# Bias rows fetched per tile and multiplied in four row tiles of TensorE, in an adaLN, scan and mixture-of-experts kernel

## The chip, the cores and the metric

The kernel runs on one core of one Trainium2 chip. The metric is the device time of one execution in microseconds. Five engines run their own instruction queues side by side: TensorE (PE, with its weight loads shown apart as PEld), VectorE (DVE), ScalarE (ACT), GpSimd (POOL), and SyncE (SP), which here only issues transfers. They are tied together by semaphores: an instruction that waits holds up everything behind it on its own queue.

## The reference

The input `x` is 16 batches of 512 tokens of 128 numbers. A first half normalises, modulates, runs a decaying scan and adds back; it takes the first 150 to 160 us of the kernel and is not touched by the change. The second half is a mixture of 8 experts with the best 2 per token:

```
h = jnp.einsum('td,edf->etf', xt, W1) + b1[:, None, :]
h = _layernorm(jax.nn.relu(h), g1, be1)
y = jnp.einsum('etf,efd->etd', h, W2) + b2[:, None, :]
y = _layernorm(jax.nn.relu(y), g2, be2)
gate = (jax.nn.one_hot(idx, E, dtype=x.dtype) * probs[..., None]).sum(axis=1)
out = jnp.einsum('te,etd->td', gate, y)
```

Here D = 128, F = 512, and `b1` is one row of 512 numbers per expert.

## The kernel before

Tokens are sorted by expert into rows in DRAM, and the second half runs over 135 expert tiles (`EXPERT_TILES`) of 128 rows, each of one expert. The code is a software pipeline written out by hand: `run_tiles` calls an `expert_step(s, n)` on each engine for s = 0, 1, 2, ..., and each engine does at step s a fixed list of jobs for tiles at different ages. The order of work on an engine is the order in which these lines are written. The jobs that matter here are these.

- **TensorE, step s.** `hidden(s)` makes h of tile s in a PSUM bank: a product of ones with `b1` (L1561), then three products of 512 columns (L1562 to L1564, high and low parts of activations and weights). Then it turns the rows of tile s+2 (L1553), makes y of tile s-4 in eight passes (L1672), and turns the activated h of tile s-2 in four (L1569).
- **ScalarE, step s.** It rounds tile s+1 (`h3hi`, L765), takes relu of h of tile s-1 (L769), relu of the normalised y of tile s-5 (`v`, L870), copies the turned h of tile s-3 (L773), and scales y of tile s-8 (`vs`, L878). In some steps it also works on finished batches (L845).
- **VectorE, step s.** It takes y of tile s-5 out of PSUM (`v0`, L1362), then does the normalisations, `h3lo`, statistics of h, and at the end the target rows of tile s (L1346).
- **GpSimd.** It adds the last shift to y of each tile (`add_shift`, L662, signals `y_ready`) and scatters the results by indirect transfers.
- **SyncE.** `load_next(i)` waits until tile i-8 has been turned and has its target rows, loads the rows of tile i (L504), and then calls `load_shifts(i - 6)`, which loads the three shift vectors of tile i-6, spread over all partitions (L515). Their buffers come round: up to tile 39 sixteen tiles later, from tile 40 on eight tiles later, and a load has to wait until GpSimd has used the buffer's last tile (the wait on `y_ready` in the lines below). Numbers of tiles and experts are loaded into registers four at a time.

```
def load_shifts(i):
    if i % AT_ONCE == 0:
        load_expert_numbers(i)
...
    if last_user(i) is not None:
        sp.wait_ge(y_ready, last_user(i) + 1)
    sp.dma_start(shift_rows[ring(i)], shifts_d[bass.ds(expert_of[i], 1), :].broadcast_to([P, 3 * D])).then_inc(shifts_loaded[shift_lane(i)], 16)
```

Before the change all of `b1` sits in SBUF (`b1_parts`, 128 partitions, high part in row 0, low part in row 1, the rest zeros written by eight ScalarE copies at the start, L747). PSUM holds h in banks 1 and 2, turned h in banks 3 and 0, y in banks 4 and 5, each pair used in turn, and turned rows in 6 and 7.

Of the kernel before, what the change touches and what calls it, by code (L numbers as in the profile page):

```python
# [6 lines left out]
def adaln_ssm_moe_kernel(nc, x_in, win_in, bin_in, bp_in, cp_in, dp_in, wout_in, bout_in, wr_in, br_in,  # L7
# [57 lines left out]
    gates_d = nc.dram_tensor("gate_b_rows", (1, B * D), F32, kind="Internal").ap()  # L65

    with ExitStack() as ctx:  # L67
# [3 lines left out]
        def sem(name):  # L71
            return ctx.enter_context(nc.semaphore(name))
# [46 lines left out]
        b1_parts = sb("b1_parts", [P, E, F], F32R)  # L119
# [160 lines left out]
        def last_user(i):  # L280

            return max((m for m in range(i) if ring(m) == ring(i)), default=None)

        early01 = [t[:].rearrange("p c l -> p (c l)").rearrange("p (j k) -> p j k", j=J) for t in xi]
# [28 lines left out]
        spare_stored = sem("spare_stored")  # L313
        pool_consts = sem("pool_consts")
        dve_setup, act_setup, pe_setup = sem("dve_setup"), sem("act_setup"), sem("pe_setup")
        gb_stored, gb_loaded, b1_stored = sem("gb_stored"), sem("gb_loaded"), sem("b1_stored")

# [18 lines left out]
        sums_done, sums_copied, sums_stored, sums_loaded, w2_ready = (  # L336
            sem("sums_done"), sem("sums_copied"), sem("sums_stored"), sem("sums_loaded"), sem("w2_ready"))
# [74 lines left out]
        def _(sp):  # L412
# [41 lines left out]
            sp.dma_start(sums_d, w2_sums).then_inc(sums_stored, 16)  # L454
            sp.dma_start(shifts_d[:, 0:D].rearrange("(o e) d -> o e d", o=1), w2_sums[0:1, :, :]).then_inc(shifts_stored, 16)
            sp.wait_ge(sums_stored, 16)
            sp.wait_ge(shifts_stored, 16)
# [3 lines left out]
            sp.wait_ge(act_setup, 3)  # L461
            sp.dma_start(b1_parts[0:1, :, :].bitcast(F32), b1hi.bitcast(F32)).then_inc(b1_stored, 16)
            sp.dma_start(b1_parts[1:2, :, :].bitcast(F32), b1lo[:].bitcast(F32)).then_inc(b1_stored, 16)

            sp.wait_ge(dve_setup, SETUP_PADDING)
            for n in range(NSPARE):
                sp.dma_start(rows_d[SPARE + n * P:SPARE + (n + 1) * P, :], padding[:]).then_inc(spare_stored, 16)
# [6 lines left out]
            sp.wait_ge(shifts_stored, 48)  # L474
# [3 lines left out]
            AT_ONCE = 4  # L478
            row_of, expert_of = {}, {}
# [95 lines left out]
            for i in range(ROUND1, EXPERT_TILES):  # L575
                if i == LAST_ROWS:
                    sp.wait_ge(spare_stored, 16 * NSPARE)
                    sp.wait_ge(padding_stored, 16 * E)
# [162 lines left out]
        def _(act):  # L741
# [3 lines left out]
            act.wait_ge(dve_setup, SETUP_PADDING)  # L745
            for e in range(E):
                ins = nc.scalar.activation(b1_parts[:, e, :], padding[:, TAGS:TAGS + 1].broadcast_to([P, F]), ACT.Copy)  # L747
            ins.then_inc(act_setup, 1)
# [18 lines left out]
            def hidden(i):  # L767
                act.wait_ge(h_done, i + 1)
                nc.scalar.activation(r[i % DEPTH], bank[1 + i % 2][:], ACT.Relu).then_inc(r_ready, 1)  # L769

            def hidden_turned(i):
                act.wait_ge(tr_done, i + 1)
                nc.scalar.activation(rT[i % DEPTH], bank[3 * (1 - i % 2)][:], ACT.Copy).then_inc(rT_ready, 1)  # L773
# [82 lines left out]
            def expert_step(s, n):  # L856
                q = n % 2
                if on(s + 1, EXPERT_TILES) and s + 1 >= EARLY_H:
                    high_part(s + 1, bank[7 - q][:, 0:P])
                if s == 1:  # L860
                    half_gates()
                if on(s - 1, EXPERT_TILES) and s - 1 >= EARLY_H:
# [24 lines left out]
                if s == EXPERT_TILES + 4:  # L887
                    late_y0g(EARLY, range(HALF, J))
# [27 lines left out]
        def _(dve):  # L916
# [52 lines left out]
            def gains_setup():  # L969
# [5 lines left out]
                dve.wait_ge(act_setup, 3)  # L975
# [381 lines left out]
            def values(s, q, p):  # L1357
# [4 lines left out]
                vec.scalar_tensor_tensor(wide(v0[p]), wide(bank[4 + p][:, 0:D]), rse[q][:, 0:1],  # L1362
# [135 lines left out]
        def _(pe):  # L1498
# [55 lines left out]

            def hidden(i):
                e, q = expert_of[i], i % 2
                h = bank[1 + q][:].rearrange("p (o f) -> p o f", o=1)
# [8 lines left out]
            def turn_hidden(i):  # L1566
                pe.wait_ge(r_ready, i + 1)
                for ch in range(CF):
                    ins = tr(bank[3 * (1 - i % 2)][:, ch * P:(ch + 1) * P], r[i % DEPTH][:, ch * P:(ch + 1) * P], ident[:])  # L1569
                ins.then_inc(tr_done, 1)  # L1570
# [83 lines left out]
            def expert_step(s, n):  # L1654
# [7 lines left out]
                if on(s - 4, EXPERT_TILES):  # L1662
                    e4 = expert_of[s - 4]
                    acc = bank[4 + q][:, 0:D].rearrange("p (o d) -> p o d", o=1)
# [70 lines left out]
```

## Time and profile before

| what | value |
|---|---|
| three timed runs | 515.19 to 515.96 us, median 515.49 us |
| profiled execution, first to last instruction (span) | 512.1 us |
| TensorE busy | 486.5 us, 95% of the span |
| VectorE busy | 440.3 us, 86% |
| ScalarE busy | 420.4 us, 82% |
| GpSimd busy | 364.3 us, 71% |
| mean granted TensorE clock | 0.985 of full speed |

The profile page gives no time for the profiled execution apart from its span; the 3.4 us between the span and the median of the timed runs lie outside the first and the last instruction. Busy shares are means over the whole kernel, so they are to be read by stage. Numbers of lines are those of the kernel before, except where rows of the change are shown.

### The profile page before, as it was taken

To read this page: it belongs to the slowest core of one execution; us is meant where nothing else is said; L and a number is where in the kernel's file an instruction comes from. 1 tells how busy PE (TensorE), PEld (TensorE's weight loads), DVE (VectorE), ACT (ScalarE), POOL (GpSimd) and SP (SyncE) were. 2 spreads that over 40 slices of the span, in tenths; PEclk is the share of its full clock that TensorE was granted. 3 is DMA by queue.
4 is the path that set the end of the run, shared out by engine and by line. 5 is a ranking of instruction groups with operands and counts; after the bars stand their busy time and mean duration, and the time that the engine had idled before them with its cause. 6 is when DMAs were issued, how large, how long until landed. Compare 5 with 4: busy or idle time off the path is not lost. (4 is left out here: it accounts for less than half of the span.)

```text
span 512.1 us, 14684 instructions
## 1 busy us (share of the span) xinstructions
PE 486.5 (95%) x3051; PEld 386.3 (75%) x3051; DVE 440.3 (86%) x2217; ACT 420.4 (82%) x1148; POOL 364.3 (71%) x483
## 2 busy tenths in 40 slices
PE   7989999999985899999999999999999999999994
PEld 6446656555544798998989799998999989999951
DVE  7779899998887698888888799988989999898894
ACT  6678887978764688888888798899989889999883
POOL 1004665666667778888888888888888888888871
PEclk9999999999997899999999999999999999999998
DMA  6980111145111789677515785677677677567555
GB/s 166 312 240 27 44 47 48 47 131 111 55 44 52 166 154 172 188 191 198 163 64 158 187 221 152 184 205 176 164 207 191 162 189 206 151 187 214 164 173 164
DMA packets 79786, 77.78 MB, mean 152 GB/s; under 512 B 11150, under 2 KB 72745, under 8 KB 79702
## 3 DMA queue, kind: packets, MB, share of 16 engines
q1 hardware_dynamic: 71286, 59.92, 47.2%
q0 software_dynamic: 8416, 16.93, 9.2%
q8 instruction: 29, 0.48, 0.3%
q14 instruction: 55, 0.45, 0.3%
HBM read 54.65 MB, written 22.59 MB: 151 GB/s over the span
## 5 line engine op out<-in xcount | busy, mean ns | idle before, releaser
L646 POOL DMA_INDIRECT expert_rows<-rows_ring,slot x128 | 123.3, 963 | 93.6 <-issue 76.3
L674 POOL DMA_INDIRECT expert_results<-y,target x119 | 123.0, 1034 | 30.7 <-issue 26.2
L1672 PE MATMUL bank<-W,h2T 128*128 x720 | 95.4, 275 | 0.8 <-ACT h2T L773 0.3
L1672 PEld LDWEIGHTS bank<-W,h2T 128*128 128x128 f32 x720 | 87.7, 192 | 9.1 <-issue 1.4
L870 ACT ACTIVATE v<-wmod 128x128 f32<-128x128 f32 x135 | 42.0, 311 | 39.1 <-DVE vg L1373 35.5
L1362 DVE SCALAR_TENSOR_TENSOR wmod<-bank,rse,shifts 128x128 f32<-128x128 f32 x119 | 41.6, 350 | 30.8 <-PE bank L1672 25.9
L1561 PE MATMUL bank<-b_parts,onesr 128*128 x135 | 64.9, 481 | 1.2 <-DVE h3lo L1140 1.2
L758 ACT ACTIVATE n<-X,nm,rs 128x128 f32<-128x128 f32 x128 | 54.1, 486 | 8.0 <-DVE nm L1307 8.0
L1145 DVE BATCH_NORM_STATS2 stf<-h1T 128x6 f32<-128x512 f32 x90 | 59.2, 658 | 0.0
L1569 PE MATMUL bank<-ident_wr,h1T 128*128 128x128 f32 x360 | 54.5, 274 | 0.0
L1562 PE MATMUL bank<-W1hi,h3hi 128*128 x135 | 53.8, 399 | 0.0
L1563 PE MATMUL bank<-W1lo,h3hi 128*128 x135 | 53.7, 398 | 0.0
L1564 PE MATMUL bank<-W1hi,h3lo 128*128 x135 | 53.6, 397 | 0.0
L769 ACT ACTIVATE h1T<-bank 128x512 f32<-128x512 f32 x90 | 53.0, 589 | 0.2 <-PE bank L1564 0.2
L773 ACT ACTIVATE h2T<-bank 128x512 f32<-128x512 f32 x90 | 52.3, 581 | 0.1
L1672 PE MATMUL bank<-W,third_rT 128*128 x360 | 47.6, 275 | 0.8 <-ACT third_rT L773 0.8
L1672 PEld LDWEIGHTS bank<-W,third_rT 128*128 128x128 f32 x360 | 43.7, 192 | 4.9 <-issue 1.0
L1569 PEld LDWEIGHTS bank<-ident_wr,h1T 128*128 128x128 f32 x360 | 42.9, 142 | 0.3 <-issue 0.2
L1373 DVE SCALAR_TENSOR_TENSOR vg<-v,mve,shifts 128x128 f32<-128x128 f32 x119 | 42.5, 357 | 0.0
L882 ACT ACTIVATE sde<-mve,eps 128x2 f32<-128x2 f32 (+1 forms) x138 | 40.6, 295 | 0.9 <-DVE mve L1386 0.7
L1140 DVE TENSOR_TENSOR h3lo<-bank,h3hi 128x128 fp32r<-128x128 f32 x135 | 37.9, 281 | 2.8 <-ACT h3hi L765 2.8
L1381 DVE BATCH_NORM_STATS2 sty<-v 128x6 f32<-128x128 f32 x135 | 38.0, 281 | 0.3 <-ACT v L870 0.2
(250 smaller groups left out, 1229.0 us busy)
## 6 DMA issues: line engine op xcount, KB each, us to landing
shifts<-expert_shifts SPq DMA_DIRECT2D x119, 192.0 KB
hrow<-expert_rows SPq DMA_DIRECT2D x135, 65.0 KB
xi<-expert_results SPq DMA_DIRECT2D x12, 512.0 KB, 5.3
out_x<-X SPq DMA_DIRECT2D x15, 256.0 KB
X<-in_L_attn_x SPq DMA_DIRECT2D x7, 512.0 KB, 7.4
W1lo<-in_L_ffn_W SPq DMA_DIRECT2D x4, 512.0 KB, 6.7
expert_rows<-rows_ring,slot POOLq DMA_INDIRECT x128
expert_results<-y,target POOLq DMA_INDIRECT x119
```

The source lines that it names most:

```text
L646: nc.gpsimd.indirect_dma_start(out=rows_d, out_offset=bass.IndirectOffsetOnAxis(ap=slot[q][:, n // TOPK, n % TOPK:n % TOPK + 1], axis=0), ...
L674: nc.gpsimd.indirect_dma_start(out=results_d, out_offset=bass.IndirectOffsetOnAxis(ap=target[i % TARGETS][:], axis=0), in_=y[k], in_offset ...
L758: ins = nc.scalar.activation(dst[:, j:j + 1, :], X[:, bass.ds(b * J + j, 1), :], ACT.Identity, bias=nm_[:, x_tiles + j:x_tiles + j + 1], s ...
L769: nc.scalar.activation(r[i % DEPTH], bank[1 + i % 2][:], ACT.Relu).then_inc(r_ready, 1)
L773: nc.scalar.activation(rT[i % DEPTH], bank[3 * (1 - i % 2)][:], ACT.Copy).then_inc(rT_ready, 1)
L1145: vec.bn_stats(stf[i % 2][:], r[i % DEPTH]).then_inc(stf_ready, 1)
L1561: mm(h, onesr[:], b1_parts[:, bass.ds(e, 1), :], start=True, stop=False)
L1562: mm(h, h3hi[i % DEPTH], W1hi[:, bass.ds(e, 1), :], start=False, stop=False)
L1563: mm(h, h3hi[i % DEPTH], W1lo[:, bass.ds(e, 1), :], start=False, stop=False)
L1564: mm(h, h3lo[i % DEPTH], W1hi[:, bass.ds(e, 1), :], start=False, stop=True).then_inc(h_done, 1)
L1569: ins = tr(bank[3 * (1 - i % 2)][:, ch * P:(ch + 1) * P], r[i % DEPTH][:, ch * P:(ch + 1) * P], ident[:])
L1672: ins = mm(acc, rT[(s - 4) % DEPTH][:, ch * P:(ch + 1) * P], W2[:, bass.ds(e4 * CF + ch, 1), :], start=(ch == 0), stop=(ch == CF - 1))
```

## The change

The two rows of `b1` of a tile (high and low part) no longer stay in SBUF. They are kept in a DRAM table `b1_d`, and each tile's two rows come by a transfer of its own into `b1_ring`, at partition 0, 32, 64 or 96 and one of two turns. The four bias products of four tiles (i to i+3, i a multiple of four) are issued one behind the other at the start of tile i, each with two rows only, in four row tiles of the array and into four h banks (1, 2, 3, 0). Turned h has one bank (4), y one bank (5). ScalarE takes relu ahead of the rounding copy in every fourth step. The zero copies at the start go, and a few semaphores are merged.

```diff
+        b1_ring = sb("b1_ring", [P, 2, F], F32R)
...
+        hidden_banks = [bank[n] for n in (1, 2, 3, 0)]
...
+        turned_bank, value_bank = bank[4], bank[5]
...
+            def load_b1(i):
+                if i == 0:
+                    sp.wait_ge(b1_stored, 32)
+                if i >= 2 * TOGETHER:
+                    sp.wait_ge(h_done, i - 2 * TOGETHER + 1)
+                for n in together(i):
+                    part, turn = b1_rows(n)
+                    sp.dma_start(b1_ring[part, turn, :].bitcast(F32), b1_d[bass.ds(expert_of[n], 1), :, :].rearrange("o k f -> (o k) f")
+                                 ).then_inc(b1_loaded[turn], 16)
+
             def load_shifts(i):
                 if i % AT_ONCE == 0:
                     load_expert_numbers(i)
-                if i == SLOTS:
-                    sp.wait_ge(b1_stored, 32)
+                if i % TOGETHER == 0:
+                    load_b1(i)
                 if last_user(i) is not None:
                     sp.wait_ge(y_ready, last_user(i) + 1)
...
-            for e in range(E):
-                ins = nc.scalar.activation(b1_parts[:, e, :], padding[:, TAGS:TAGS + 1].broadcast_to([P, F]), ACT.Copy)
...
+                last_of_group = s % TOGETHER == 0
+                if last_of_group and on(s - 1, EXPERT_TILES) and s - 1 >= EARLY_H:
+                    hidden(s - 1)
                 if on(s + 1, EXPERT_TILES) and s + 1 >= EARLY_H:
                     high_part(s + 1, bank[7 - q][:, 0:P])
...
+            def biases(i):
+                pe.wait_ge(b1_loaded[i // TOGETHER % 2], b1_count(i))
+                pe.wait_ge(r_ready, i)
+                for n in together(i):
+                    part, turn = b1_rows(n)
+                    mm(hidden_bank(n)[:], onesr[part, :], b1_ring[part, turn, :], start=True, stop=False)
...
-                if i >= 2:
-                    pe.wait_ge(r_ready, i - 1)
-                mm(h, onesr[:], b1_parts[:, bass.ds(e, 1), :], start=True, stop=False)
...
+                pe.wait_ge(rT_ready, i)
...
-                    if on(s - 6, EXPERT_TILES):
-                        pe.wait_ge(v0_ready, s - 5)
+                    if on(s - 5, EXPERT_TILES):
+                        pe.wait_ge(v0_ready, s - 4)
```

On SyncE the queue in the later tiles, where every fourth step loads four expert numbers (`experts`), reads like this before the change; `hrow` are a tile's rows, `shifts` its shift vectors.

```order
L515 DMA shifts<-expert_shifts 128x384
L504 ISA [waits target_ready,t3_done]
L504 DMA hrow<-expert_rows 128x130
L490 TENSOR_LOAD experts
L515 ISA [waits y_ready]
L515 DMA shifts<-expert_shifts 128x384
```

With the change four loads into `b1_ring` stand in the same place, behind the shift load of the tile before (with its wait on `y_ready`) and behind the row load of six tiles ahead.

```order
L549 ISA [waits y_ready]
L549 DMA shifts<-expert_shifts 128x384
L528 ISA [waits target_ready,t3_done]
L528 DMA hrow<-expert_rows 128x130
L514 TENSOR_LOAD experts
L539 ISA [waits h_done]
L539 DMA b_ring<-b_two_parts 2x512
L539 ISA
L539 DMA b_ring<-b_two_parts 2x512
L539 ISA
L539 DMA b_ring<-b_two_parts 2x512
```

The fourth such load and the tile's own shift load follow. So the loads for tiles i to i+3 are issued after the shift load of tile i-1.

On TensorE one tile begins like this before the change: the turns of the tile two steps back (L1569), the bias product, the products with `W1`.

```order
L1569 MATMUL bank<-ident_wr,h1T 128x128 [waits r_ready]
L1569 MATMUL bank<-ident_wr,h1T 128x128 x3
L1561 ISA [waits r_ready,h3lo_ready]
L1561 MATMUL bank<-b_parts,onesr 128x512
L1562 REGISTER_ALU
L1562 MATMUL bank<-W1hi,h3hi 128x512
```

With the change every fourth tile begins with four bias products that wait for the loads and for the relu of all tiles before, and the other three tiles begin with the products of `W1`.

```order
L1611 MATMUL bank<-ident_wr,h1T 128x128 [waits rT_ready,r_ready]
L1611 MATMUL bank<-ident_wr,h1T 128x128 x3
L1593 MATMUL bank<-b_ring,onesr 128x512 [waits r_ready,b1_loaded0]
L1593 MATMUL bank<-b_ring,onesr 128x512 x3
L1603 ISA [waits h3lo_ready]
L1603 MATMUL bank<-W1hi,h3hi 128x512
```

The first of the four carries the wait on `b1_loaded`, which counts all four loads of the group.

## Rows read from the trace of the kernel before

**Rows 1.** The page: span, and the busy time of the engines.

```profile
span 512.1 us, 14684 instructions
...
PE 486.5 (95%) x3051; PEld 386.3 (75%) x3051; DVE 440.3 (86%) x2217; ACT 420.4 (82%) x1148; POOL 364.3 (71%) x483
```

**Rows 2.** Waits of the engines, whole kernel: engine, line, releaser, us, times, longest.

```profile
DVE wmod L1362 <- PE bank L1672: 29.6, 72, 1.4
```

**Rows 3.** Timeline of TensorE, one step (tile 58) and the next bias: start, us, what.

```profile
302.69 0.47 PE L1561 MATMUL bank<-b_parts,onesr 128*128 x1
...
303.00 0.39 PE L1562 MATMUL bank<-W1hi,h3hi 128*128 x1
...
303.24 0.40 PE L1563 MATMUL bank<-W1lo,h3hi 128*128 x1
...
303.81 1.06 PE L1672 MATMUL bank<-W,h2T 128*128 x8
...
305.06 0.48 PE L1561 MATMUL bank<-b_parts,onesr 128*128 x1
```

**Rows 4.** Timeline of the other engines around the same step.

```profile
301.44 1.06 PE L1672 MATMUL bank<-W,third_rT 128*128 x8
...
302.54 0.35 DVE L1362 SCALAR_TENSOR_TENSOR wmod<-bank,rse,shifts 128x128 f32<-128x128 f32 x1
...
304.00 0.39 ACT L878 ACTIVATE wmod<-vg,rse 128x128 f32<-128x128 f32 x1
...
304.27 0.24 DVE L1346 TENSOR_SCALAR target<-hrow,tile_e 128x1 int32<-128x1 f32 x1
...
304.48 0.45 POOL L662 TENSOR_TENSOR y<-wmod,shifts 128x128 f32<-128x128 f32 x1 [0.40 <-ACT wmod L878]
...
305.04 0.59 ACT L769 ACTIVATE h1T<-bank 128x512 f32<-128x512 f32 x1
```

**Rows 5.** Waits of SyncE's queue, whole kernel: line, releaser, us, times, longest.

```profile
SPq L515 <- POOL y L662: 96.4, 85, 9.9
SPq L521 <- DVE target L1346: 74.8, 27, 47.1
```

**Rows 6.** Timeline of SyncE's transfers, in the later tiles.

```profile
305.08 0.33 SPq L515 DMA_DIRECT2D shifts<-expert_shifts  x1
305.65 0.33 SPq L504 DMA_DIRECT2D hrow<-expert_rows  x1
```

**Rows 7.** Timeline of SyncE's transfers, in the earlier tiles.

```profile
208.31 0.33 SPq L504 DMA_DIRECT2D hrow<-expert_rows  x1
209.15 0.33 SPq L515 DMA_DIRECT2D shifts<-expert_shifts  x1
210.65 0.33 SPq L504 DMA_DIRECT2D hrow<-expert_rows  x1
211.17 0.33 SPq L515 DMA_DIRECT2D shifts<-expert_shifts  x1
```

**Rows 8.** DMA issues: transfer, count, KB each, median us from issue to landing.

```profile
y<-in_L_c SPq DMA_DIRECT2D x1, 8.0 KB, 1.5
...
boutc<-in_L_attn_bout SPq DMA_DIRECT2D x1, 0.5 KB, 2.2
...
expert_rows<-padding SPq DMA_DIRECT2D x15, 65.0 KB, 3.0
```

**Rows 9.** Windows of TensorE: us, busy us (count), granted clock, DMA share, GB/s.

```profile
152.40:155.90 3.50, 0.93 (x11) 0.50 0.15 49
155.90:159.40 3.50, 3.50 (x12) 0.54 0.18 59
159.40:160.40 1.00, 0.76 (x5) 1.00 0.20 67
```

**Rows 10.** Timeline of TensorE at the end of the first half; in brackets the idle time before.

```profile
151.07 0.66 PE L1539 MATMUL bank<-ident_wr,mixT_both 128*128 128x128 f32 x4 [1.93 <-ACT mixT_both L820]
```

**Rows 11.** Waits of ScalarE in the first 30 us, from the timeline.

```profile
10.49 0.78 ACT L805 ACTIVATE h1T<-bank,mod 128x512 f32<-128x512 f32 x1 [1.27 <-DVE gb_raw L966]
```

More of the change, by code:

```diff
@@ L65, in adaln_ssm_moe_kernel @@
     gates_d = nc.dram_tensor("gate_b_rows", (1, B * D), F32, kind="Internal").ap()
+    b1_d = nc.dram_tensor("b1_two_parts", (E, 2, F), F32, kind="Internal").ap()
     with ExitStack() as ctx:
@@ L118, in adaln_ssm_moe_kernel @@
         b1hi = third_rT[0:E, :]
-        b1_parts = sb("b1_parts", [P, E, F], F32R)
+        TOGETHER = 4
+        QUARTER = P // TOGETHER
+        b1_ring = sb("b1_ring", [P, 2, F], F32R)
         onesr = sb("onesr", [P, P], F32R)
@@ L282, in last_user, with together, b1_rows, b1_count @@
             return max((m for m in range(i) if ring(m) == ring(i)), default=None)
+        def together(i):
+            return range(i, min(i + TOGETHER, EXPERT_TILES))
+        def b1_rows(i):
+            first = i % TOGETHER * QUARTER
+            return slice(first, first + 2), i // TOGETHER % 2
+        def b1_count(i):
+            return 16 * sum(len(together(n)) for n in range(i % (2 * TOGETHER), i + 1, 2 * TOGETHER))
+        hidden_banks = [bank[n] for n in (1, 2, 3, 0)]
+        def hidden_bank(i):
+            return hidden_banks[i % len(hidden_banks)]
+        turned_bank, value_bank = bank[4], bank[5]
         early01 = [t[:].rearrange("p c l -> p (c l)").rearrange("p (j k) -> p j k", j=J) for t in xi]
@@ L316, in adaln_ssm_moe_kernel @@
         gb_stored, gb_loaded, b1_stored = sem("gb_stored"), sem("gb_loaded"), sem("b1_stored")
+        b1_loaded = [sem(f"b1_loaded{n}") for n in range(2)]
         (n1_ready, t1_done, h1T_ready, xi0_done, xi1_done, xi0_ready, xi1_ready, z_done,
@@ L453, in _ @@
             sp.wait_ge(sums_copied, 2)
-            sp.dma_start(sums_d, w2_sums).then_inc(sums_stored, 16)
+            sp.dma_start(sums_d, w2_sums).then_inc(shifts_stored, 16)
             sp.dma_start(shifts_d[:, 0:D].rearrange("(o e) d -> o e d", o=1), w2_sums[0:1, :, :]).then_inc(shifts_stored, 16)
-            sp.wait_ge(sums_stored, 16)
-            sp.wait_ge(shifts_stored, 16)
+            sp.wait_ge(shifts_stored, 32)
             sp.dma_start(means[:, 0:E, :], sums_d[1:2].broadcast_to([P, E, D])).then_inc(sums_loaded, 16)
             sp.wait_ge(dve_setup, SETUP_END)
-            sp.wait_ge(act_setup, 3)
-            sp.dma_start(b1_parts[0:1, :, :].bitcast(F32), b1hi.bitcast(F32)).then_inc(b1_stored, 16)
-            sp.dma_start(b1_parts[1:2, :, :].bitcast(F32), b1lo[:].bitcast(F32)).then_inc(b1_stored, 16)
+            sp.wait_ge(act_setup, 2)
+            sp.dma_start(b1_d[:, 0, :], b1hi.bitcast(F32)).then_inc(b1_stored, 16)
+            sp.dma_start(b1_d[:, 1, :], b1lo[:].bitcast(F32)).then_inc(b1_stored, 16)
             sp.wait_ge(dve_setup, SETUP_PADDING)
             for n in range(NSPARE):
-                sp.dma_start(rows_d[SPARE + n * P:SPARE + (n + 1) * P, :], padding[:]).then_inc(spare_stored, 16)
+                sp.dma_start(rows_d[SPARE + n * P:SPARE + (n + 1) * P, :], padding[:]).then_inc(padding_stored, 16)
             for n, src in ((0, g2_in), (1, be2_in)):
@@ L473, in _ @@
                 sp.dma_start(shifts_d[:, (1 + n) * D:(2 + n) * D], second_gains[n]).then_inc(shifts_stored, 16)
-            sp.wait_ge(shifts_stored, 48)
+            sp.wait_ge(shifts_stored, 64)
             sp.wait_ge(w1lo_ready, E)
@@ L478, in _ @@
             AT_ONCE = 4
+            assert TOGETHER == AT_ONCE
             row_of, expert_of = {}, {}
@@ L576, in _ @@
                 if i == LAST_ROWS:
-                    sp.wait_ge(spare_stored, 16 * NSPARE)
-                    sp.wait_ge(padding_stored, 16 * E)
+                    sp.wait_ge(padding_stored, 16 * (NSPARE + E))
                     rows_of_batches(B)
@@ L861, in expert_step @@
                     half_gates()
-                if on(s - 1, EXPERT_TILES) and s - 1 >= EARLY_H:
+                if not last_of_group and on(s - 1, EXPERT_TILES) and s - 1 >= EARLY_H:
                     hidden(s - 1)
@@ L974, in gains_setup @@
                 assert done[0] == SETUP_SUMS
-                dve.wait_ge(act_setup, 3)
+                dve.wait_ge(act_setup, 2)
                 mark(vec.tensor_tensor(b1lo[:], b1f[:], b1hi, ALU.subtract))
@@ L1553, in turn_rows @@
                 tr(to, hrow[row_slot][:, H], ident[:]).then_inc(t3_done, 1)
-            def hidden(i):
-                e, q = expert_of[i], i % 2
-                h = bank[1 + q][:].rearrange("p (o f) -> p o f", o=1)
+            def biases(i):
[4 more added lines that the diff above has]
+                    mm(hidden_bank(n)[:], onesr[part, :], b1_ring[part, turn, :], start=True, stop=False)
+            def hidden(i):
+                e = expert_of[i]
+                h = hidden_bank(i)[:].rearrange("p (o f) -> p o f", o=1)
+                if i == 0:
+                    pe.wait_ge(h3lo_ready, EARLY_H)
+                if i % TOGETHER == 0:
+                    biases(i)
                 pe.wait_ge(h3lo_ready, i + 1)
-                if i >= 2:
-                    pe.wait_ge(r_ready, i - 1)
-                mm(h, onesr[:], b1_parts[:, bass.ds(e, 1), :], start=True, stop=False)
                 mm(h, h3hi[i % DEPTH], W1hi[:, bass.ds(e, 1), :], start=False, stop=False)
```

17 lines of the change are left out of this document (7 added, 10 removed).

## The prediction

> **What bounds the kernel now.** I read the page first: TensorE is busy 95% of the span, the others less [rows 1]. Then the waits: VectorE waits for TensorE's y in 72 tiles, 29.6 us in all [rows 2], so the tile phase runs at TensorE's pace and the other engines follow it. Then the timeline of one step: from one bias product to that of the next tile 302.69 to 305.06, 2.37 us [rows 3], and the 135 tiles keep that step almost throughout. A group of four tiles takes 9.48 us. What the change touches besides TensorE is SyncE's queue, so I read its waits too: it is not idle in the sense of being early. Its shift loads wait 85 times for GpSimd's add, 96.4 us in all, and its row loads 27 times for the target rows of VectorE [rows 5]. So whatever is put into this queue behind these waits is issued at their pace, not ahead of it. Until now that did no harm: shift vectors are used five steps later, rows six.
>
> **What it saves on TensorE.** The bias product costs 302.69 to 303.00, 0.31 us, of which 0.07 is the weight load that any first product after the turns pays (the next product follows after 0.24, 303.00 to 303.24) [rows 3]. So a step without it takes 2.37 - 0.24 = 2.13. Each group adds once a cost c for the four bias products. No row shows row tiles. From below c is one product, 0.24; from above it is four, one behind the other, 0.95, and twice the part of a product that goes on after the next has started (0.39 - 0.24 = 0.15, [rows 3]) if the array is emptied on both sides: 1.25. I take c = 0.45, one product and three more exposed weight loads of 0.07, nearer the lower end because the four have separate rows and banks. Then the group is 4 x 2.13 + 0.45 = 8.97 of TensorE, 0.5 less than now.
>
> The Trainium skill (TensorE: Matmul & The Clock Gate, Measured speedup vs the span model) has four row tiles of 32 rows and 512 columns at 3.07 times the speed of four in a row; c would be 0.95 / 3.07 = 0.31 by it and the sum 33 x 0.14 = 5 us less. Against the change speaks the Trainium skill (TensorEngine Tiling (Array Packing), Key Properties): changing the tiling mode drains TensorE. With both drains priced at 0.15 on top of 0.45 the sum would be 33 x 0.30 = 10 us more.
>
> **What it adds: the loads of b1 come late.** The four loads of group S (tiles S to S+3) stand behind the row load of tile S+6 and the shift load of tile S-1, and the first product of step S waits for all four. I follow the chain from the start of one group to that of the next.
>
> From tile 40 on the shift load of tile S-1 waits for the add of tile S-9, which ScalarE and GpSimd do late in their step S-1. In the rows: y of step 57 ends at 301.44 + 1.06 = 302.50, VectorE takes it at 302.54, ScalarE scales at 304.00, GpSimd adds at 304.48 [rows 4], and the shift load of tile 58 leaves at 305.08 [rows 6], when TensorE starts tile 59 (305.06, [rows 3]). Behind it: 0.57 to the row load (305.08 to 305.65, [rows 6]); 0.84 from there to the next transfer where expert numbers are read in between (208.31 to 209.15), and 0.52 from one issue to the next (210.65 to 211.17) for three more loads [rows 7]; and the landing of the last. Landing from issue: 1.5 us for 8 KB, 2.2 for 0.5 KB, 3.0 for 65 KB [rows 8]. These loads are 4 KB; I take 2.2 and keep 1.5 and 3.0 for the range. From the start of group S to the end of y in step S+2: c, two steps of 2.13, and 302.69 to 303.81 + 1.06 less 0.24, 1.94 [rows 3], together 6.20 + c = 6.65. Then 302.50 to 305.08, 2.58; then 0.57 + 0.84 + 3 x 0.52 = 2.97; then 2.2. The sum is 14.40 us from group to group, against 9.48 now. TensorE has 8.97 of work in it and stands for 5.4.
>
> Up to the group of tile 40 the shift buffers come round after sixteen tiles and their wait is over; what holds the queue is the row load of tile S+6, which waits for the target rows of tile S-2. That is one step earlier: 4.07 + c = 4.52 to the end of y in step S+1; 302.50 to the end of the target rows at 304.51 is 2.01 [rows 4], and 0.15 to the load (as from GpSimd's add, 304.93, to the shift load); then 0.84 + 1.56 and 2.2. Together 11.28, with 2.3 us of standing.
>
> **The clock.** After an idle stretch of 1.93 us [rows 10] the granted clock went to 0.50, 1.2 GHz, and stayed there for 3.5 us after TensorE was at work again, 155.9 to 159.4, before it was 1.00 [rows 9]. At half clock 3.5 us do the work of 1.75. A stand of 5.4 us is well beyond that; I charge 1.8 per group. For 2.3 us I charge half, 0.9, since one row of that size is no proof for all. Behind these rows stands the Trainium skill (TensorE: Matmul & The Clock Gate, HAM oscillation — how this bites in real kernels): a wait for a transfer in every tile makes every tile begin at the lower clock. Were that so for the early groups too, they would lose 1.8 each and the sum be 9 us more.
>
> **What costs nothing.** The relu wait: a group needs relu of tile S-1, which runs 305.04 to 305.63 beside a bias at 305.06 [rows 3, 4]; 0.5 us late if the loads were early, hidden wholly behind a stand of 2.3 or 5.4, and if the loads were in time it would be the next wait. The single banks for turned h and y wait for copies that end during the stand as well. The eight zero copies at the start sit before a wait of ScalarE for VectorE of 1.27 us [rows 11], so their going frees nothing. The wait on `h_done` in front of the loads is for a tile eight back, long done. The extra bytes, 4 KB per tile, are small beside 65 KB of rows and the shift vectors.
>
> **The sum.** Groups 4 to 40 are 10, groups 44 to 132 are 23; group 0 is loaded long before. Late groups: 14.40 + 1.8 - 9.48 = 6.72, times 23 is 154.6. Early groups: 11.28 + 0.9 - 9.48 = 2.70, times 10 is 27. Together 181.6 us on a span of 512.1, or on the median of 515.5 (3.4 us lie outside the span and stay): **697 us**.
>
> **The rivals.**
> - *The loads are late, but the clock holds.* For it: one row of a fall after a short stand is little, and 8.97 us of dense work stand between the stands. Without the clock the sum loses 23 x 1.8 + 10 x 0.9 = 50: 647 us.
> - *The clock stays down for whole groups.* Then 6.65 of the chain doubles in late groups (4.85 more each than charged), and in early groups TensorE's 8.97 doubles to 17.9 and sets the pace itself (5.7 more each): 112 + 57, 866 us. Against it: after 3.5 us of steady work the clock came back [rows 9].
> - *Dearer pieces.* Landing at 3.0 adds 33 x 0.8 = 26; c at 1.25 adds 33 x 0.8 = 26: 723 each, 749 both. Landing at 1.5 takes 23 off.
> - *The loads are in time.* Then it is not slower. That decides itself at one point: the last load must land before the first product of step S, some 5 us earlier than the chain gives, which needs the adds of GpSimd two steps earlier than in rows 4 and 6. Then the group is 8.97 and the relu wait of 0.45, 9.42 against 9.48: 33 x 0.06, 513.5 us, no change. The 85 waits of rows 5 speak against it.
>
> **Chances and range.** The forecast 0.55, clock holds 0.18, dearer pieces 0.16, clock down for good 0.08, in time 0.03. A difference under 0.2% can't be told from none here; faster gets 0.01, same 0.02, slower 0.97. The range takes the forecast, the clock that holds with short landings (down to 630) and the dear pieces together (up to 755), and leaves out the last two.
>
> **What would show it.** TensorE waits before the first bias product of nearly every group, some 2 us in early groups and 5 in late ones, released by the `b1_ring` loads; steps are about 2.1 within a group; SyncE's shift loads still wait for GpSimd; the granted clock falls after the stands; the bias group itself is short, about 0.45. The forecast is wrong if the loads land before the group, if their landing is far from 2.2 us, or if the clock does not fall.

## The result and the profile after

The changed kernel takes 700.21 us (median of four runs, 696.45 to 703.36), the kernel before 515.34 us beside it on the same chip (four runs, 514.96 to 515.96). The ratio is 1.358, with a 95% interval of 1.354 to 1.362. The profiled execution has a span of 698.7 us, 186.6 more than before, and a mean granted TensorE clock of 0.867 against 0.985.

The page of the changed kernel answers to [rows 1] and says at once that no engine got more work. TensorE and VectorE are busy for 63 and 1 us more, in a span that is 187 us longer:

```profile
span 698.7 us, 14981 instructions
PE 549.2 (79%) x3051; PEld 424.2 (61%) x3051; DVE 441.2 (63%) x2217; ACT 419.0 (60%) x1140; POOL 360.3 (52%) x483
```

The waits of the changed kernel (engine, line, releaser, total us, times, longest) answer to [rows 2] and [rows 5]. First TensorE, then VectorE, then SyncE's queue:

```profile
PE bank L1593 <- DMA b_ring<-b_two_parts: 126.5, 33, 6.7
DVE wmod L1395 <- PE bank L1714: 214.6, 86, 9.4
SPq L549 <- POOL y L695: 208.5, 68, 8.7
```

TensorE waits 33 times, once for every group but the first, for the new loads. 126.5 us of these waits and 63 us more of busy time make up the 187 us to within 3 us. The count of instructions is that of before, so the 63 us are the same work done slower. SyncE still waits for GpSimd's add, 208.5 us instead of 96.4, and VectorE for TensorE: everything stands in one ring.

The timeline of TensorE over one late group, from the bias products of tile 92 to those of tile 96 (start, us, engine, line, operation; in brackets the idle time before and its releaser):

```profile
499.74 0.80 PE L1593 MATMUL bank<-b_ring,onesr 2*128 2x512 f32 x4 [4.35 <-DMA b_ring<-b_two_parts]
500.47 0.80 PE L1603 MATMUL bank<-W1hi,h3hi 128*128 x1
...
504.55 0.78 PE L1603 MATMUL bank<-W1hi,h3hi 128*128 x1
...
507.59 0.48 PE L1603 MATMUL bank<-W1hi,h3hi 128*128 x1
...
508.48 1.06 PE L1714 MATMUL bank<-W,h2T 128*128 x8
...
509.73 0.47 PE L1603 MATMUL bank<-W1hi,h3hi 128*128 x1
...
516.77 0.80 PE L1593 MATMUL bank<-b_ring,onesr 2*128 2x512 f32 x4 [4.65 <-DMA b_ring<-b_two_parts]
```

and SyncE's transfers in the same stretch, which answer to [rows 6]:

```profile
512.25 0.33 SPq L549 DMA_DIRECT2D shifts<-expert_shifts  x1
512.82 0.33 SPq L528 DMA_DIRECT2D hrow<-expert_rows  x1
513.66 1.57 SPq L539 DMA_DIRECT2D b_ring<-b_two_parts  x4
...
515.00 0.24 SPq L539 DMA_DIRECT2D b_ring<-b_two_parts  x1
```

The last row, from a narrower window, is the fourth of the b1 loads by itself. The order is the one foretold: y of step S+2 (508.48 + 1.06 = 509.54), the add, the shift load at 512.25, the row load, the four b1 loads, and 1.77 us after the last of them was issued TensorE's next group. The windows of TensorE in this group (us, busy us and count, granted clock, DMA share, GB/s) answer to [rows 9]:

```profile
499.70:503.60 3.90, 3.86 (x15) 0.50 0.30 66
503.60:507.20 3.60, 3.60 (x19) 0.60 0.00 0
507.20:512.10 4.90, 4.90 (x38) 1.00 0.56 145
512.10:516.77 4.67, 0.02 (x2) 1.00 0.80 258
```

The first two steps, 4.08 and 3.04 us (500.47, 504.55, 507.59), run wholly or for the greater part at half clock; the third is 2.14.

An early group begins otherwise. The timeline of TensorE, tiles 20 and 24:

```profile
227.35 0.51 PE L1593 MATMUL bank<-b_ring,onesr 2*128 2x512 f32 x4 [1.53 <-DMA b_ring<-b_two_parts]
227.79 0.50 PE L1603 MATMUL bank<-W1hi,h3hi 128*128 x1
...
230.85 1.05 PE L1714 MATMUL bank<-W,third_rT 128*128 x8
...
238.05 0.51 PE L1593 MATMUL bank<-b_ring,onesr 2*128 2x512 f32 x4 [1.42 <-DMA b_ring<-b_two_parts]
```

and SyncE's in front of the second of them:

```profile
234.12 0.33 SPq L528 DMA_DIRECT2D hrow<-expert_rows  x1
234.96 1.75 SPq L539 DMA_DIRECT2D b_ring<-b_two_parts  x4
...
236.30 0.41 SPq L539 DMA_DIRECT2D b_ring<-b_two_parts  x1
```

All ten early groups (tiles 4 to 40) start their bias products at full clock (0.50 or 0.51 us for the four) after stands of 1.3 to 2.5 us; of the 23 late ones (tiles 44 to 132), after stands of 4.0 to 6.7 us, 20 take 0.80, the duration at half clock, and three 0.64 to 0.66.

### The profile page after: what moved, and what is told of

Its sections match the earlier page's. It is cut to its first block and busy times, and to the rows that moved or that the text cites. A ratio compares the mean times of both kernels' runs of the same rounds, so it can differ in the third digit from the quotient of the medians.

```text
span 698.7 us, 14981 instructions
## 1 busy us (share of the span) xinstructions
PE 549.2 (79%) x3051; PEld 424.2 (61%) x3051; DVE 441.2 (63%) x2217; ACT 419.0 (60%) x1140; POOL 360.3 (52%) x483
## 5 line engine op out<-in xcount | busy, mean ns | idle before, releaser
L1593 PE MATMUL bank<-b_ring,onesr 2*128 2x512 f32 x135 | 23.8, 689 | 126.5 <-DMA b_ring<-b_two_parts 126.5
L795 ACT ACTIVATE h3hi<-bank 128x128 fp32r<-128x128 f32 x135 | 35.9, 267 | 135.8 <-PE bank L1586 135.6
L1714 PE MATMUL bank<-W,h2T 128*128 x720 | 110.5, 304 | 0.5 <-DVE wmod L1395 0.4
L1714 PEld LDWEIGHTS bank<-W,h2T 128*128 128x128 f32 x720 | 103.0, 220 | 11.7 <-issue 6.0
L1593 PEld LDWEIGHTS bank<-b_ring,onesr 2*128 2x128 f32 x135 | 8.6, 244 | 134.7 <-DMA b_ring<-b_two_parts 132.7
L1603 PE MATMUL bank<-W1hi,h3hi 128*128 x135 | 79.5, 589 | 0.6 <-DVE h3lo L1173 0.6
L695 POOL TENSOR_TENSOR y<-wmod,shifts 128x128 f32<-128x128 f32 x58 | 28.5, 493 | 88.0 <-ACT wmod L911 87.7
L1604 PE MATMUL bank<-W1lo,h3hi 128*128 x135 | 63.2, 468 | 0.0
L1605 PE MATMUL bank<-W1hi,h3lo 128*128 x135 | 62.3, 461 | 0.0
L695 POOL TENSOR_TENSOR y<-win,shifts 128x128 f32<-128x128 f32 x28 | 13.9, 496 | 84.6 <-ACT win L911 84.5
```

The lines of the kernel that those rows point to most:

```text
L695: nc.gpsimd.tensor_tensor(wide(y[k]), wide(vs[i % VS]), wide(shift_rows[k][:, 2 * D:3 * D]), ALU.add).then_inc(y_ready, 1)
L1603: mm(h, h3hi[i % DEPTH], W1hi[:, bass.ds(e, 1), :], start=False, stop=False)
L1604: mm(h, h3hi[i % DEPTH], W1lo[:, bass.ds(e, 1), :], start=False, stop=False)
L1605: mm(h, h3lo[i % DEPTH], W1hi[:, bass.ds(e, 1), :], start=False, stop=True).then_inc(h_done, 1)
L1714: ins = mm(acc, rT[(s - 4) % DEPTH][:, ch * P:(ch + 1) * P], W2[:, bass.ds(e4 * CF + ch, 1), :], start=(ch == 0), stop=(ch == CF - 1))
```

## Experiments

The theory: the time is lost because the b1 loads stand in SyncE's queue behind two waits, and because TensorE's clock is down after each stand. The main rivals: the loads themselves are the cost wherever they stand, the four row tiles or the single banks cost it, or the clock has no share. Medians below are beside 515.2 to 515.5 us of the kernel before.

**Loads one group early (`ahead`).**

```diff
+                if i == 0:
+                    load_expert_numbers(0)
+                    load_b1(0)
-                if i % AT_ONCE == 0:
-                    load_expert_numbers(i)
-                if i % TOGETHER == 0:
-                    load_b1(i)
+                if i % AT_ONCE == 0 and i + AT_ONCE < EXPERT_TILES:
+                    load_expert_numbers(i + AT_ONCE)
+                    load_b1(i + TOGETHER)
```

> The four bias loads of a group are issued one group earlier in SyncE's queue, in front of the shift load of tile S-4, with the expert numbers read one group earlier as well; nothing else differs from the change. Theory (the time went into standing for loads that are issued late, and into the lower clock after each stand): the stands of 1.4 and 4.3 to 6.7 us go, the clock stays at 1.00, a group takes 8.97 plus a relu wait of some 0.45, 9.4 us, and the kernel about 514 us (508 to 522). Rival A (SyncE or the transfer queues have too much to do with 135 more transfers): the stands stay in part, over 560 us. Rival B (the four row tiles themselves slow TensorE down): no stands, but products of twice the length and over 560 us.

Measured: 522.14 us, ratio 1.0147 (1.0097 to 1.0196). 178 of the 185 us are gone with the b1 loads, and the read of the expert numbers that they need, moved up in SyncE's queue. So lateness is the cause of nearly all of it, and not the transfers, the row tiles or the banks. But it is slower than before, and just beyond the range expected (508 to 522). TensorE's waits in it:

```profile
PE bank L1595 <- ACT h1T L801: 7.8, 21, 0.7
PE bank L1595 <- ACT decay L801: 4.0, 11, 0.7
```

The four products need relu of tile S-1, and 32 of 33 groups now wait for it. Groups take 9.49 to 10.5 us. That is more than these waits explain, and the later runs were made for it.

**Sixteen shift buffers for all tiles, loads left late (`buffers16`).**

```diff
+        more_shifts = sb("more_shifts", [P, SLOTS, 3 * D])
+        shift_rows += [more_shifts[:, n, :] for n in range(SLOTS)]
...
-                if last_user(i) is not None:
-                    sp.wait_ge(y_ready, last_user(i) + 1)
-                sp.dma_start(shift_rows[ring(i)], ...
+                if i >= 2 * SLOTS:
+                    sp.wait_ge(y_ready, i - 2 * SLOTS + 1)
+                sp.dma_start(shift_rows[i % (2 * SLOTS)], ...
```

> The bias loads stay where the change has them, but the shift vectors get sixteen buffers for all tiles, so that the shift load of tile S-1 waits for the add of tile S-17 and no longer for that of tile S-9. Theory (the wait of the shift load for GpSimd's add in front of the bias loads makes the late groups, from tile 44 on, so slow): late groups become like the early ones of the change, 10.6 to 12.3 us instead of 16.6, so 23 x 5.2 = 120 us less, about 580 us (570 to 592), with stands of 1.4 us. Rival (the stand comes from the landing of the loads, or from the number of transfers, not from that wait): the late groups keep over 15 us, over 660 us.

Measured: 569.19 us (one run), just under the 570 to 592 expected. The mean late group (tiles 40 to 132) goes from 16.57 to 10.96 us, somewhat less than the early groups' 11.60. The wait for GpSimd's add is no longer among SyncE's, and the wait for the target rows has taken its place, as the early part of the prediction says:

```profile
SPq L556 <- DVE target L1380: 143.5, 58, 46.4
```

**Loads late, TensorE kept at work (`busy`).** From tile 44 on, TensorE runs sixteen products of no use before it waits for the loads.

```diff
+                if i >= 44:
+                    pe.wait_ge(v0_ready, i - 4)
+                    for _ in range(16):
+                        mm(value_bank[:], onesr[:], W1hi[:, 0, :], start=True, stop=True)
                 pe.wait_ge(b1_loaded[i // TOGETHER % 2], b1_count(i))
```

> Bias loads as late as in the change, but in the groups from tile 44 on TensorE passes the stand with 16 products of 512 columns into the y bank that nobody reads, after VectorE has taken y out of it. Theory (a good part of a late group, some 2.7 us, is the lower clock after the stand): the clock stays at 1.00, a late group takes 13.9 us instead of 16.6, and the kernel 23 x 2.7 = 62 us less, about 638 us (630 to 650). Rival (the longer products after a stand are due to the row tiles or to the transfers, not to idleness): about 700 us.

Measured: 653.67 us (one run), 46.5 less with more work, but above the 630 to 650 expected. The timeline of TensorE shows the filling, a remaining wait of 0.28 us, and a group that starts at full clock:

```profile
411.85 4.00 PE L1592 MATMUL bank<-W1hi,onesr 128*128 128x512 f32 x16
416.12 0.50 PE L1597 MATMUL bank<-b_ring,onesr 2*128 2x512 f32 x4 [0.28 <-DMA b_ring<-b_two_parts]
```

The mean late group is 14.71 us; the prediction's chain without the clock is 14.40. So some 1.9 us of the mean late group were the clock's, and more than that in all, since some groups lose it still: after a wait of 2.43 us at 400.91 the step behind it is 3.77 us long (W1 products at 401.35 and 405.12), the next 2.14 again. That is why the gain fell short of the 2.7 us a group expected.

**No row tiles (`ahead_one_row_tile`).** As `ahead`, with all four pairs of rows at partitions 0 and 1.

```diff
-        b1_ring = sb("b1_ring", [P, 2, F], F32R)
+        b1_ring = sb("b1_ring", [P, 2 * TOGETHER, F], F32R)
...
-            return slice(first, first + 2), i // TOGETHER % 2
+            return slice(0, 2), i % (2 * TOGETHER)
```

> As the run with the loads one group ahead, but all four bias rows lie at partitions 0 and 1, so that the four products of a group use the same row tile and can't run side by side. Theory (four row tiles run side by side, c = 0.45): the four products now take 0.95 to 1.15 us, 0.5 to 0.7 more per group, 34 groups, 17 to 24 us more than the run beside it, about 535 us. Rival (the products run one behind the other in either case): the same time as the run beside it.

Measured: 548.81 us, ratio 1.0643 (1.0609 to 1.0677), 26.7 us over `ahead`, where 17 to 24 were expected. The timeline has the four one behind the other, 1.08 us to the next product where row tiles take 0.44:

```profile
240.20 1.16 PE L1594 MATMUL bank<-b_ring,onesr 2*128 2x512 f32 x4 [0.32 <-ACT h1T L800]
241.28 0.50 PE L1604 MATMUL bank<-W1hi,h3hi 128*128 x1
```

So the row tiles do run side by side, and save 0.64 us a group against the same rows in one tile. That is 21 of the 26.7 us; a part of the rest is clock, which in this profiled execution is at 0.50 for 24 us between 145 us and tile 8, against 17 in `ahead`, and again in two later groups.

**Is relu's wait what is left?** Four kernels, all with the loads early. `ahead_order_before` lets ScalarE do the rounding copy before relu in every step. `ahead_fourth_later` issues the fourth bias product behind the first tile's W1 products. `ahead_three` and `ahead_two` take three or two tiles together, so that relu of tile S-1 is not needed; ScalarE is in the order of before.

```diff
# ahead_order_before
-                last_of_group = s % TOGETHER == 0
+                last_of_group = False
# ahead_fourth_later
-                for n in together(i):
+                for n in together(i)[:TOGETHER - 1]:
...
                 mm(h, h3lo[i % DEPTH], W1hi[:, bass.ds(e, 1), :], start=False, stop=True).then_inc(h_done, 1)
+                if i % TOGETHER == 0 and i + TOGETHER - 1 < EXPERT_TILES:
+                    if i:
+                        pe.wait_ge(r_ready, i)
+                    bias(i + TOGETHER - 1)
# ahead_three (ahead_two: TOGETHER = 2)
-        TOGETHER = 4
+        TOGETHER = 3
...
-                pe.wait_ge(r_ready, i)
+                if i >= len(hidden_banks):
+                    pe.wait_ge(r_ready, i + TOGETHER - len(hidden_banks))
```

> As the run 'ahead' (loads of b1 one group early, 522.1 us), but ScalarE keeps the order of the kernel before in every step: rounding copy of tile s+1 first, relu of tile s-1 behind it. Theory (the group of four needs relu of tile S-1, and that wait is what is left in 'ahead'): relu comes later by the rounding copy, 0.26 us a piece, and its wait, so a group start waits 0.3 to 0.5 us longer in each of 33 groups: 532 us (527 to 540). Rival (what is left in 'ahead' is ScalarE or VectorE being full, wherever relu stands): 520 to 524 us.

> As 'ahead', but the fourth bias product of a group is issued after the three W1 products of the group's first tile, alone, so that the other three need relu of tile S-2 only. Theory (relu wait): in 'ahead' steps within a group are 2.14 us and only the step before a group start is longer (2.62 in all with the bias, up to 3.3); without the wait a group is 4 x 2.14 + 0.44 + 0.24 = 9.24 instead of 9.5 to 10.2, so 522 - 33 x 0.26 - some 8 x 0.6 = 509 us (505 to 515). Rival (VectorE and ScalarE, busy 86 to 91% of the time in the kernel before at 2.37 us a step, can't follow at 2.3): the wait appears elsewhere and the time stays at 518 to 524 us.

> As 'ahead', but three tiles together in three row tiles, four h banks as before, ScalarE in the order of the kernel before. Three products need the banks of tiles i-4 to i-2 only, so relu of tile i-1 is not waited for. Theory (relu wait): three steps are 3 x 2.14 + 0.44 = 6.86 us, 2.29 a tile against 2.44 (mean of 'ahead' from 173 to 485 us): 135 x 0.15 = 20 less, 502 us, and up to 510 if ScalarE holds some steps up (500 to 512). Rival (engines full): 515 to 522 us.

> As 'ahead_three' with two tiles together. Two products need the banks of tiles i-4 and i-3, no wait at all; two steps are 2 x 2.14 + 0.35 to 0.44 = 4.63 to 4.72 us, 2.34 a tile against 2.37 in the kernel before: 522 - 135 x 0.10 = 508 us (505 to 516) by the theory of the relu wait; rival (engines full): 515 to 522 us. If both 'ahead_three' and 'ahead_two' come to their estimates, three is the faster by some 6 us.

Measured: 530.57 us (ratio 1.0277, 1.0241 to 1.0314), 528.69 (1.0259, 1.0236 to 1.0283), 515.23 (1.000, 0.9987 to 1.0013) and 540.01 (1.0478, 1.0458 to 1.0497). The first is as the relu theory says. The other three are not: the wait for relu is gone from all of them, yet they gain less than expected or lose. Two tiles together are far worse than three, which no full engine explains. A part of that is loads that are late again, since a group of two is loaded only two tiles ahead; TensorE's wait in `ahead_two`:

```profile
PE bank L1597 <- DMA b_ring<-b_two_parts: 8.4, 9, 2.2
```

After three of these waits the clock falls too, and the next groups take 6.52 us instead of 4.91. The timelines show what else was left out. `ahead_three`, from the turns of one step over three bias products to the next turns and products:

```profile
302.07 0.60 PE L1615 MATMUL bank<-ident_wr,h1T 128*128 128x128 f32 x4
302.60 0.51 PE L1597 MATMUL bank<-b_ring,onesr 2*128 2x512 f32 x3
303.04 0.50 PE L1607 MATMUL bank<-W1hi,h3hi 128*128 x1
...
304.84 0.60 PE L1615 MATMUL bank<-ident_wr,h1T 128*128 128x128 f32 x4
305.19 0.48 PE L1607 MATMUL bank<-W1hi,h3hi 128*128 x1
```

and `ahead_fourth_later`, its three products and its single one:

```profile
302.58 0.60 PE L1621 MATMUL bank<-ident_wr,decay 128*128 128x128 f32 x4
303.11 0.51 PE L1599 MATMUL bank<-b_ring,onesr 2*128 2x512 f32 x3
303.55 0.49 PE L1609 MATMUL bank<-W1hi,h3hi 128*128 x1
...
304.44 0.49 PE L1599 MATMUL bank<-b_ring,onesr 2*128 2x512 f32 x1
...
305.92 0.60 PE L1621 MATMUL bank<-ident_wr,h1T 128*128 128x128 f32 x4
```

Without a bias the next product starts 0.35 us after the turns began (304.84 to 305.19). With one, the bias starts after 0.53 and W1 0.44 later: 0.62 us for three products, 0.18 of it an empty gap ahead of them, with no wait recorded. From turns to turns the step with the bias takes 2.77 (302.07 to 304.84), where a step without takes 2.14: again 0.63. A single product costs nearly the same. The step of `ahead_fourth_later` with three products and the single one takes 3.34 (302.58 to 305.92), 1.20 more than 2.14, which leaves 0.58 for the single one. And two: the undisturbed groups of `ahead_two` have a period of 4.91 us (bias products at 207.01 and 211.92), which is 2 x 2.14 + 0.63. The cost is that of going to two-row products and back, and hardly depends on how many there are.

Two of the misses add up with it. In the profiled execution of `ahead_two`, 25 of the 30 us above the kernel before lie between tiles 8 and 132, and of these 62 groups at 4.91 instead of 2 x 2.37 make 10.5, the waits for loads 8.4, and the clock behind three of them 3 x 1.6. In that of `ahead_fourth_later` 9 of the 11 us lie there: 31 groups at 9.78 instead of 9.48.

**Three full-row products (`three_full_rows`).** As `ahead_three`, with the same loads, waits and banks, but the products use all 128 rows. The ring is zeroed at the start, and every h gets the sum of the rows of three tiles in place of its own bias.

```diff
-                    mm(hidden_bank(n)[:], onesr[part, :], b1_ring[part, turn, :], start=True, stop=False)
+                    mm(hidden_bank(n)[:], onesr[:], b1_ring[:, turn, :], start=True, stop=False)
```

> As 'ahead_three' (515.2 us), but the three bias products use all 128 rows, no row tiles; the ring is zeroed first, so each h gets the sum of the rows that the ring holds for three tiles: the bias is changed, the output too. Theory (the 0.63 us of a group are the change into row tiles and back): the first product starts 0.36 us after the turns before it began instead of 0.53, three products cost 3 x 0.24, a period of three steps is 3 x 2.14 + 0.72 = 7.14 instead of 7.05, and the time 45 x 0.09 = 4 us more: 519 us. Rival (the 0.17 us in front of the products come from their waits or from the banks): the 0.53 stay, the period is 7.3 and the time 527 us.

Measured: 518.99 us, ratio 1.0074 (1.0050 to 1.0098), 3.8 us over `ahead_three`. The timeline:

```profile
302.61 0.60 PE L1617 MATMUL bank<-ident_wr,h1T 128*128 128x128 f32 x4
302.96 0.94 PE L1599 MATMUL bank<-b_ring,onesr 128*128 128x512 f32 x3
303.74 0.39 PE L1609 MATMUL bank<-W1hi,h3hi 128*128 x1
...
305.43 0.49 PE L1617 MATMUL bank<-ident_wr,h1T 128*128 128x128 f32 x3
```

The bias starts 0.35 us after the turns, without the gap. The gap belongs to the row tiles, not to the waits or the banks. Three products take 0.78 to the first W1 product, but that product then costs 0.09 less than it does behind the turns (0.23 to the next, 303.74 to 303.97, against 0.32 from 305.19 to 305.51 in `ahead_three`). So the whole step is the measure: 2.82 here (302.61 to 305.43; the median of such steps is 2.83) against 2.77 in row tiles. Three full-row products cost 0.69, three in row tiles 0.63; 45 groups make 3 us of that difference, and 3.8 were measured. Two would be dearer in row tiles.

**A fifth h bank (`ahead_five_banks`, `five_banks_relu_first`, `five_banks_turned_early`).** Four tiles together without the wait for relu of tile S-1. All rows are turned into one bank, which moves that turn to the end of the step. The second kernel lets ScalarE take relu ahead of the rounding copy in every step; the third also copies turned h before relu v.

```diff
-        hidden_banks = [bank[n] for n in (1, 2, 3, 0)]
+        hidden_banks = [bank[n] for n in (1, 2, 3, 0, 7)]
...
                     turn_hidden(s - 2)
+                if on(s + 2, EXPERT_TILES):
+                    pe.wait_ge(h3lo_ready, s + 2)
+                    turn_rows(s + 2, bank[6][:, 0:P])
# five_banks_relu_first
-                last_of_group = False
+                last_of_group = True
# five_banks_turned_early, besides (the later copy of turned h goes)
-                if on(s - 3, EXPERT_TILES) and s >= EXPERT_TILES:
+                if on(s - 3, EXPERT_TILES) and s > 3:
                     hidden_turned(s - 3)
```

> As 'ahead' (four tiles together, loads one group early), with a fifth h bank, so that the four products need relu of tile S-2 only; the bank is won by turning the rows of all tiles into one bank instead of two, which moves that turn to the end of the step, behind the rest of h3 of the tile before. ScalarE in the order of the kernel before. Theory from 'ahead', 'ahead_three', 'ahead_two' and 'ahead_fourth_later': four steps without bias are 4 x 2.14, a change into row tiles and back costs 0.63 us whatever the number of products, the rest of 'ahead' was the relu wait. So a group is 9.19 against 9.48 before: 33 x 0.29 = 10 less, 506 us (502 to 512). Rival (VectorE and ScalarE hold steps up below 2.37 us): 513 to 518. Second rival (the turn at the end of the step is too late, a wait for h3lo in each step): over 520.

> As 'ahead_five_banks' (526.3 us, steps of 2.37 us in which ScalarE waits 126 times for the rows that are turned at the end of the step), but ScalarE takes relu of tile s-1 ahead of the rounding copy in every step, so that it does something while the rows are turned. Theory (a loop: turn of rows, rounding copy, relu, copy of turned h, next turn of h, turn of rows): the loop loses relu's 0.59 us, falls below TensorE's own 2.14, and a group is 9.19: 506 us (502 to 512). Rival (VectorE and ScalarE are full below 2.37): 513 to 520. If the loop is elsewhere: 524 to 528.

> As 'five_banks_relu_first', and ScalarE copies turned h of tile s-3 ahead of relu v of tile s-5, so that the one bank for turned h comes free without v's waits for VectorE. Theory: if the copy of turned h is what TensorE's turns still wait for, 2 to 8 us under 'five_banks_relu_first'; if not, the same, or some us more where v then comes late for VectorE.

Measured: 526.29 us (ratio 1.0215, 1.0184 to 1.0246), 517.40 (1.0053, 1.0031 to 1.0074) and 516.31 (1.0019, 1.0005 to 1.0032). The first fell to its second rival. Its steps are 2.37 us, very evenly, because ScalarE waits in nearly every one for the late turn:

```profile
ACT h3hi L797 <- PE bank L1588: 57.9, 126, 1.5
```

Relu first breaks that loop, but under half of what was expected came, and the time lies where the rival of full engines put it (513 to 520). The third kernel is only 1.1 us under the second, where 2 to 8 were expected if the copy of turned h was what TensorE's turns waited for. The windows of `five_banks_relu_first` over four groups each, early and late (us; busy us and count of PE, PEld, DVE, ACT and POOL; granted clock, DMA share, GB/s):

```profile
201.93:238.66 36.73, 36.73 (x273) 32.93 (x272) 32.42 (x145) 31.46 (x98) 30.76 (x40) 1.00 0.74 191
433.12:471.68 38.56, 38.42 (x273) 32.86 (x272) 34.33 (x153) 34.01 (x105) 30.97 (x50) 1.00 0.60 171
```

Up to tile 44 most groups take 9.18 us, as worked out (9.19). In the late stretch it is 9.64, with VectorE busy 89% and ScalarE 88%, and the two waiting for each other (28.6 us of VectorE for the rounding copy in 81 steps, 28.2 of ScalarE for VectorE's statistics in 87). Which order of work would let them follow is open. No version tried here is faster than the kernel before; `ahead_three` equals it.

## Why the prediction was right, and where it was off

**The mechanism** is as told: the loads wait behind the shift load from tile 40 on and behind the row load before, a group cannot start until they land, and the clock falls in the late stands or right behind them. `ahead` shows the first, `buffers16` the change between the two stages, `busy` the clock's share. Term by term, for the two groups shown:

| late group (tiles 92 to 96) | forecast | measured |
|---|---|---|
| start to end of y in step S+2, with the clock | 6.65 + 1.8 = 8.45 | 9.80 (499.74 to 509.54) |
| to the shift load | 2.58 | 2.71 |
| to the row load, to the first b1 load | 0.57 + 0.84 | 0.57 + 0.84 |
| three more loads | 1.56 | 1.34 |
| landing of the last | 2.2 | 1.77 |
| sum | 16.20 | 17.03 (mean of 23: 16.57) |

| early group (tiles 20 to 24) | forecast | measured |
|---|---|---|
| start to end of y in step S+1 | 4.52 | 4.55 (227.35 to 231.90) |
| to the row load | 2.16 | 2.22 |
| to the first b1 load | 0.84 | 0.84 |
| three more loads | 1.56 | 1.34 |
| landing of the last | 2.2 | 1.75 |
| clock | 0.9 | 0 |
| sum | 12.18 | 10.70 (mean of nine, tiles 4 to 40: 11.60) |

(The landing is taken from the issue of the last load, 515.00 and 236.30, to the start of TensorE's products.)

**The clock was sized too low for late groups.** The prediction charged 1.8, from 3.5 us at half clock after the end of the first half. In the group shown the clock stayed at 0.50 for the better part of two steps, until about 506.5, and y came 3.15 us later than the 6.65 of full clock. Over the 23 late groups TensorE worked for 3.4 to 6.8 us at 0.50 behind the stand, 5.5 on average, so the charge should have been 2.8 a group instead of 1.8. The size came from a misreading of [rows 9]. The clock of the kernel before is at 0.50 there from 152.4 on, some 7 us in all, and TensorE stands a second time in the middle of it:

```profile
155.88 2.15 PE L1629 MATMUL bank<-ident_wr,h2T 128*128 128x136 f32 x8 [2.58 <-DVE placed L1285]
```

The 3.5 us are only what came after this second stand. In the late groups a part of the stretch at half clock can fall into the stand, where it costs nothing. The windows around the longest stand, in front of tile 72:

```profile
410.02:414.30 4.28, 0.00 (x1) 1.00 0.81 211
414.40:416.72 2.32, 0.00 (x0) 0.50 0.89 264
416.72:421.10 4.38, 4.38 (x18) 0.50 0.03 7
```

The issues and the landing were sized too high by 0.65 together, and the errors nearly cancel: 23 x (16.57 - 9.48) = 163 for the late groups against 155, and 10 x (11.60 - 9.48) = 21 for the early ones against 27. That 697 came within 4 us of 700.21 is in part luck. In early groups 0.9 as a mean was near, but as a mixture: four of the nine have periods of 10.59 to 10.70 and lose nothing; four of 12.26 to 13.40 are longer by 1.6 to 2.7 us, begin at full clock and lose it at work; and one, 11.48, keeps its clock and stands for longer (2.20). The windows of the group of tile 28 (248.69, a period of 12.26, after a stand of 1.37):

```profile
248.70:250.40 1.70, 1.70 (x12) 1.00 0.70 195
250.60:253.90 3.30, 3.30 (x15) 0.50 0.92 209
254.00:257.00 3.00, 3.00 (x26) 1.00 0.84 208
```

The Trainium skill (TensorE: Matmul & The Clock Gate, HAM oscillation — how this bites in real kernels) describes a kernel in which every tile's wait for a transfer is longer than its work, and every tile then starts at the lower clock. The late groups agree, 20 of 23 with bias products at 0.80, though their stands are shorter than their work; after stands of 1.3 to 2.5 us no group began so.

**Row tiles.** c = 0.45 held in the changed kernel: 227.35 to 227.79 is 0.44. But only because the gap ahead of the products, 0.18, lies in the stand there, and not for the reason given: the four take 0.51 us together where one alone takes 0.49 (`ahead_fourth_later`), so they run at once and no three further pieces of 0.07 come between them. The size of c was luck. Where TensorE does not stand it is 0.62. The rival of loads in time used 8.97 for a group, which is 9.19 then, and 0.45 for relu; beyond 9.19 a group of `ahead` takes 0.3 at the least (9.49) and up to 1.3, with waits for relu of 0.2 to 0.7 recorded; what else makes the longest groups is not shown. So that rival's 513.5 was 522.1, on the side of slower. The cost that the prediction named beside c as a rule, and priced at 0.30 more, is there, at 0.17 more. The Trainium skill (TensorEngine Tiling (Array Packing), Key Properties) has it that a change of tiling mode drains TensorE. These runs agree with it as far as timing can: a cost per change that is nearly the same for one to four products (0.58 to 0.63) and goes with the row tiles. They do not show what the array does in the gap.

**The clock as a rival.** "The clock holds" gave 647; with the clock mostly held, `busy` has 653.67. By the prediction's own terms its range would run from 624 (647 less 23 for short landings) to 749, not from 630 to 755; the result lies well inside either.

## What to carry to other kernels

Before adding a transfer to an in-order queue, find which waits already stand there and when they end; a wait that did no harm for loads used five steps later decides the pace for loads used at once, and issuing them one group earlier gave back 178 of 185 us. Count a change into row tiles and back as a price per visit, here some 0.62 us against 0.23 for one full product: three products just pay, four pay more, two lose. And the dependence that the batching adds (four banks that must all be free) is a wait of its own, which shows only when the larger one is gone.

## What the runs showed of the hardware

A set of one to four two-row products between full ones costs 0.58 to 0.63 us, about the same for any number; 0.18 of it is a gap that the waits do not show. Four in separate row tiles take 0.44 us to the next product, in one tile 1.08. After stands of 4 us and more TensorE worked for 3.4 to 6.8 us at half clock, and it could lose its clock in the middle of steady work, 1.7 to 1.9 us after a stand of 1.37 us. Four loads of 4 KB left SyncE 0.42 to 0.48 us apart, and TensorE's products began 1.75 and 1.77 us after the issue of the last.
